# Row maximum negated by the masking operation, and the rotary product kept in the projection's PSUM bank

## The reference

```python
xn = layernorm(x)                                  # (4, 256, 512)
q = rope((xn @ wq).reshape(B, S, 32, 128), pos)    # 32 query heads
k = rope((xn @ wk).reshape(B, S, 8, 128), pos)     # 8 key/value heads, 4 query heads each
v = (xn @ wv).reshape(B, S, 8, 128)
scores = q @ k.T * 128 ** -0.5                     # per head
scores = where((j <= i) & (j > i - 128), scores, lowest)
s = (softmax(scores) @ v).reshape(B, S, 4096) @ wo
g = silu(w2(silu(xn @ W1.T) * (xn @ W3.T)))        # W1, W2, W3 from packed 4-bit values
out = x + s * g
```

## Time and profile before

| | |
|---|---|
| median of 3 runs | 923.35 us (922.11 to 925.94) |
| span of the profiled execution | 921.7 us |
| TensorE busy | 857.1 us, 93% |
| VectorE busy | 673.2 us, 73% |
| ScalarE busy | 471.5 us, 51% |
| GpSimd busy | 288.3 us, 31% |
| mean granted TensorE clock | 0.995 |

### The profile page before, as it was taken

How to read it: one execution, slowest core, us unless ns; L and a number is a source line. 1 busy time by engine, 2 the same in 40 slices (tenths; PEclk the granted TensorE clock), 3 DMA queues, 4 the chain that set the end, 5 groups by cost and what they waited for, 6 DMA issues and landing times.

```text
span 921.7 us, 14123 instructions
## 1 busy us (share of the span) xinstructions
PE 857.1 (93%) x4252; PEld 701.7 (76%) x4252; DVE 673.2 (73%) x1765; ACT 471.5 (51%) x1133; POOL 288.3 (31%) x223
## 2 busy tenths in 40 slices
PE   4999999999889998999999999989998999999877
PEld 3877888887677787878777777878787877778666
DVE  7954444425687969796978788597969787976994
ACT  2383112133675646565664756465747547564641
POOL 0153111124253222423321432043232314421862
PEclk9999999999999999999999999999999999999998
DMA  6100002002012001201010120012010201100111
GB/s 185 54 24 2 13 20 66 0 1 69 1 46 69 1 15 33 69 1 46 20 48 0 46 68 0 0 46 68 0 46 0 68 0 46 58 11 0 58 57 58
DMA packets 40224, 32.55 MB, mean 35 GB/s; under 512 B 5056, under 2 KB 32384, under 8 KB 40192
## 3 DMA queue, kind: packets, MB, share of 16 engines
q1 hardware_dynamic: 40192, 32.16, 12.0%
HBM read 30.05 MB, written 2.10 MB: 35 GB/s over the span
## 4 chain that ended last, share of the span: by engine, by line
PE 50%; DVE 33%; issue 11%; ACT 5%; DMA 1%; DVEq 0%; POOL 0%; ACTq 0%; SPq 0%
PE bank L992 15%; PE bank L994 15%; PE bank L993 15%; DVE probs L831 6%; DVE q L788 4%; DVE nmx L803 4%; DVE q L780 3%; DVE probs L819 3%; PE bank L1132 2%; DVE pl L837 2%; ACT oh L525 1%; DVE k L788 1%; DVE ol L848 1%; DVE ql L793 1%; DVE vl L842 1%
## 5 line engine op out<-in xcount | busy, mean ns | idle before, releaser
L322 POOL TENSOR_TENSOR swap<-swap,cst 128x512 f32<-128x512 f32 x80 | 106.8, 1334 | 369.7 <-ACT swap L485 369.7
L992 PE MATMUL bank<-xh,wih 128*128 128x512 f32 x384 | 159.3, 415 | 15.4 <-DVE q L780 15.4
L994 PE MATMUL bank<-xh,wil 128*128 128x512 f32 x384 | 151.0, 393 | 0.0
L993 PE MATMUL bank<-xl,wih 128*128 128x512 f32 x384 | 150.3, 392 | 0.0
L512 ACT ACTIVATE probs<-probs,nmx 128x128 f32<-128x128 f32 (+1 forms) x256 | 113.9, 446 | 57.1 <-DVE nmx L803 56.7
L992 PE MATMUL bank<-woh,oh 128*128 128x512 f32 x256 | 101.4, 396 | 10.3 <-DVE ol L848 10.3
L520 ACT ACTIVATE ph<-bank 128x512 fp32r<-128x512 f32 x96 | 55.6, 598 | 104.3 <-PE bank L1132 103.6
L831 DVE TENSOR_SCALAR probs<-probs,rinv 128x128 f32<-128x128 f32 (+1 forms) x256 | 99.4, 430 | 4.6
L994 PE MATMUL bank<-woh,ol 128*128 128x512 f32 x256 | 99.8, 390 | 0.0
L993 PE MATMUL bank<-wol,oh 128*128 128x512 f32 x256 | 99.7, 390 | 0.0
L992 PEld LDWEIGHTS bank<-xh,wih 128*128 128x128 f32 x384 | 72.2, 188 | 34.6 <-DVE q L780 14.5
(11 more groups left out here) (103 smaller groups left out, 1846.9 us busy)
## 6 DMA issues: line engine op xcount, KB each, us to landing
raw<-in_L_attn_wq SPq DMA_DIRECT2D x32, 256.0 KB, 2.8
raw<-in_L_attn_wo SPq DMA_DIRECT2D x32, 256.0 KB, 2.9
packed<-in_L_ffn_w SPq DMA_DIRECT2D x20, 128.0 KB, 2.1
xn<-in_L_attn_x SPq DMA_DIRECT2D x8, 256.0 KB, 3.6
raw<-in_L_attn_wk SPq DMA_DIRECT2D x8, 256.0 KB, 2.9
raw<-in_L_attn_wv SPq DMA_DIRECT2D x8, 256.0 KB, 2.6
raw<-in_L_attn_x SPq DMA_DIRECT2D x8, 256.0 KB, 2.7
out<-gate SPq DMA_DIRECT2D x8, 256.0 KB, 2.0
```

What stands on the lines that cost most here:

```text
L322: nc.gpsimd.tensor_tensor(v, v, spread(sin.unsqueeze(1), P, 2, SEQ), ALU.mult).then_inc(sin_done, 1)
L992: nc.tensor.matmul(out_, sh, mh, start=(i == 0), stop=False)
L993: nc.tensor.matmul(out_, sh, ml, start=False, stop=False)
L994: m = nc.tensor.matmul(out_, sl, mh, start=False, stop=(i == n - 1))
```

## The change

Two edits are made, both in the attention part.

The row maximum. The masking operation had scale 1, the maximum as reduction, and `NEG` as its start value. It now has scale minus `SM` (the softmax scale), the minimum as reduction, and `TOP` as start value, so that the masked scores stand in `probs` negated and scaled, and its accumulator is the bias itself. The exponential then has scale -1. `negate`, the tile `mx` and the semaphore `nmax_done` are gone; ScalarE waits for `masked`. Each head now has a memset of `pace`, where before each second one had it.

The rotary product. `cos_part` writes its product back into the projection's bank instead of into `q` or `k`. `rotate` reads the bank and `swap` and writes `q` or `k`. A projection that takes over the bank therefore waits for `rope_done`, the sum, where it waited for `cos_done`, the product.

```diff
+TOP = 3.0e38
...
             def exps(g, bp, b, h):
                 s = 4 * b + h
-                act.wait_ge(nmax_done, cnt(8, g, bp, s + 1))
+                act.wait_ge(masked, cnt(8, g, bp, s + 1))
                 for i, (c0, c1) in enumerate(((0, P), (P, 3 * P))):
                     e = nc.scalar.activation(probs[:, s, c0:c1], probs[:, s, c0:c1], ACT.Exp,
-                                             bias=nmx[:, s, i:i + 1], scale=SM, accum_out=rsum[:, s, i:i + 1])
+                                             bias=nmx[:, s, i:i + 1], scale=-1.0, accum_out=rsum[:, s, i:i + 1])
...
                 dve.wait_ge(swapped, cnt(5, g, bp, c + 1))
+                v = PJ_B[(c + 1 if c else 0) % 2][:, :].rearrange("p (b n) -> p b n", b=2)
+                nc.vector.tensor_tensor(v, v, spread(cos.unsqueeze(1), P, 2, SEQ), ALU.mult).then_inc(cos_done, 1)
+
+            def rotate(g, bp, c):
+                dve.wait_ge(sin_done, cnt(5, g, bp, c + 1))
+                dve.wait_ge(cos_done, cnt(5, g, bp, c + 1))
                 if c == 0:
                     wait(dve, scores_ps, cnt(8, g, bp, -8))
                 dst = q[:, c - 1, :] if c else k[:, bp, :]
-                nc.vector.tensor_tensor(dst.rearrange("p (b n) -> p b n", b=2),
-                                        PJ_B[(c + 1 if c else 0) % 2][:, :].rearrange("p (b n) -> p b n", b=2),
-                                        spread(cos.unsqueeze(1), P, 2, SEQ), ALU.mult).then_inc(cos_done, 1)
-
-            def rotate(g, bp, c):
-                dve.wait_ge(sin_done, cnt(5, g, bp, c + 1))
-                dve.wait_ge(cos_done, cnt(5, g, bp, c + 1))
-                dst = q[:, c - 1, :] if c else k[:, bp, :]
-                nc.vector.tensor_tensor(dst, dst, swap[:, (5 * bp + c) % 2, :], ALU.add).then_inc(rope_done, 1)
+                nc.vector.tensor_tensor(dst, PJ_B[(c + 1 if c else 0) % 2][:, :], swap[:, (5 * bp + c) % 2, :],
+                                        ALU.add).then_inc(rope_done, 1)
...
-            def negate(g, bp, b, h):
-
-                s = 4 * b + h
-                dve.wait_ge(masked, cnt(8, g, bp, s + 1))
-                nc.vector.tensor_scalar(nmx[:, s, :], mx[:, s, :], -SM, None, ALU.mult).then_inc(nmax_done, 1)
...
                     dve.wait_ge(scores_ps, cnt(8, g, bp, s + 1))
-                    if h > h0:
-                        negate(g, bp, b, h0)
-                    else:
-                        nc.vector.memset(pace[:, s // 2:s // 2 + 1], 0.0)
+                    nc.vector.memset(pace[:, s:s + 1], 0.0)
                     for i, (c0, c1) in enumerate(((0, P), (P, 3 * P))):
                         m = nc.vector.tensor_tensor_reduce(
-                            out=probs[:, s, c0:c1], in0=S_B[s % 2][:, c0:c1], in1=mask[:, c0:c1], scale=1.0,
-                            scalar=NEG, op0=ALU.add, op1=ALU.max, accum_out=mx[:, s, i:i + 1])
+                            out=probs[:, s, c0:c1], in0=S_B[s % 2][:, c0:c1], in1=mask[:, c0:c1], scale=-SM,
+                            scalar=TOP, op0=ALU.add, op1=ALU.min, accum_out=nmx[:, s, i:i + 1])
                     m.then_inc(masked, 1)
-                negate(g, bp, b, h0 + 1)
...
                     r = {0: -1, 1: 0, 2: 1, 4: 2, 5: 3}[c]
-                    wait(pe, cos_done, cnt(5, g, bp, r))
+                    wait(pe, rope_done, cnt(5, g, bp, r))
```

More of the change, by code:

```diff
@@ L119, in build @@
         vl = sb("vl", [P, 2, IT // P, HD], f32r, main)
-        mx = sb("mx", [P, 2 * GH, 2], f32, main)
-        pace = sb("pace", [P, 4], f32, main)
+        pace = sb("pace", [P, 2 * GH], f32, main)
         nmx = sb("nmx", [P, 2 * GH, 2], f32, main)
@@ L153, in build @@
         ffn_ps, ffn_read, gate_done = sem("ffn_ps"), sem("ffn_read"), sem("gate_done")
-        scores_ps, masked, nmax_done, exp_done, rinv_done, probs_done = (
-            sem("scores_ps"), sem("masked"), sem("nmax_done"), sem("exp_done"), sem("rinv_done"),
-            sem("probs_done"))
+        scores_ps, masked, exp_done, rinv_done, probs_done = (
+            sem("scores_ps"), sem("masked"), sem("exp_done"), sem("rinv_done"), sem("probs_done"))
         proj_ps, cos_done, swapped, sin_done, rope_done = (
```

## The result

The changed kernel takes 947.82 us (median of 4 runs, 946.93 to 950.8), the kernel before 924.55 in runs on the same chip: a ratio of 1.0263, interval 1.0237 to 1.0289, so 23 us slower; the forecast was 944. The profiled execution took 947.73 us with a span of 945.6.

The account below looks back on a forecast made before the run. TensorE was taken as the bound, busy 857.1 of 921.7 us. Narrow steps 16.4, wide 3.6, start 2.2, end -1 gave +21.2; with 921.7 and 1.65 around the span, 944 us, 8 in 10 for 929 to 962.

Parts of the forecast that it names:

- The three waits: Projects 2, 4 and 5 wait for rotary sums 0, 1 and 2: 1.0, 1.95 and 1.1 us late, 4.05 per step.
- The unblocked query sum: On VectorE, the query sum reading bank and swap takes 0.68 us instead of 1.28: 38 us less over 64.
- no late ol, pl or probabilities: In attend and output projection, waits for pl and ol go; 0.3 us for probabilities is kept in wide steps.
- The seven narrow steps: Steps with bp = 1: 4.05 us delay added, 1.7 removed, +2.35 each, times 7, 16.4 us.
- The wide steps: Steps with bp = 0: 4.05 + 0.3 us added, 3.9 removed, +0.45 each, times 8, 3.6 us.
- rival C: TensorE's clock falls too behind the longest wait: 1.5 us lost per step, 966 us in all; chance 10%.
- The start: Ahead of the first step: project 2 +1.5 us for the key sum, sums 1 and 2 another 0.7; 2.2.
- The end: Last group, without projections behind it: shorter VectorE work gives back an estimated 1 us.
- next to nothing of the 80 us: VectorE sheds some 80 of 673 us, but has slack, so next to nothing is on TensorE's path by itself.
- A: VectorE's relief wins: sums come early enough that new waits only replace the old cosine waits; 900 us, chance 6%.
- B: They balance: new waits of some 2.6 us per step, wide gains paying narrow losses; 922 to 928, chance 9%.
- D: Query sum still blocked: project 5 waits another 0.6 us, pl and ol stay late; 966 us, chance 4%.

Follow-up runs that it names:

- The early sums: The changed kernel with sum 0 issued ahead of both ol, sum 1 ahead of the last two normalises and vl, sum 2 ahead of pl: 885.02 us, ratio 0.9578.
- The mask edit alone: The kernel before with only the negations removed and the reduction turned round, rotary part as it was: 877.10 us, ratio 0.9489.
- the exchange of two instructions: The kernel before with vl and rotary sum 1 exchanged in VectorE's order, negations kept, nothing removed: 887.90 us, ratio 0.9604.
- the padding copy: The kernel before with negations removed and reduction turned round, plus one unread 128x512 VectorE copy per step ahead of vl: 909.01 us, ratio 0.9851.
- the rotary edit alone: The kernel before with product into the bank, sum from the bank and wait for the sum; negations as before: 972.25 us, ratio 1.0501.
- the waits alone: The kernel before with one line changed, projections waiting for rope_done (the sum) instead of cos_done (the product): 984.45 us, ratio 1.0649.

## Why the prediction was right, and what it missed

**The three waits: right.** The forecast was idle time near 0.8, 1.7 and 0.9 us ahead of projects 2, 4 and 5; the profile has 0.94 to 0.95, 1.77 to 1.78 and 0.87 to 0.96. The experiment with the one changed line shows that this edit brings them. The early sums show who sets each: the ol pair for the key sum, the last normalises and vl for sum 1 (its wait goes when it is issued ahead of them), pl for sum 2, whose wait falls to 0.40 when it goes ahead of pl (run only together with the other two).

**The unblocked query sum, no late ol, pl or probabilities: right.** 681 ns against 0.68 taken, and VectorE at 609.6 us against "near 595"; what I left out is kl, held in the sum's stead by (1061 - 706) x 16 = 5.7 us, the 64 further memsets, 3.8 us (priced below 0.1 each and then not added), and the normalises, 4.1 us longer in all. The product into PSUM at 696 ns stands by the lower of my two bounds.

**The terms.** I measured each step from the turns of v of one step to those of the next, before and after. The seven narrow steps went to 43.84 on average (forecast 43.7). Before they are not all alike: four took 41.3 and three 42.4, these with one more wait for ol of 0.8 to 0.9. So the term is 14.5 instead of 16.4 us; the sum was made on one narrow step, and the windows of all seven would have shown it. The earlier trace rows also leave out a wait of 0.29 us before project 4 in the wide steps. The wide steps (seven by this measure, the eighth lies in the end) cost 5.2 us where the forecast has 3.2 for seven. Five of them, at 43.8 to 44.0 us, are 0.1 to 0.4 longer. The other two took 45.3, with the clock at 0.96 over the step: rival C happened twice, at 1.4 us each, near the 1.5 priced. The start cost 2.8 (2.2 forecast), with the clock at 0.57 in 255 to 259 us, whose price no run separates. The end cost 1.5 where I had -0.6 (the eighth wide step's 0.45 less the 1 given back): the error there is in the sign, from the 5.32 us wait, 0.69 before, and the lower clock behind it. 2.8 + 14.5 + 5.2 + 1.5 = 24.0, and the spans differ by 945.6 - 921.7 = 23.9. The forecast of +21.2 is 2.7 us short of it. That it is so near is in part luck: the narrow steps cost 1.9 less than forecast, the two falls of the clock in the wide ones 2.8 more. The step lengths themselves, 43.84 and 43.8 to 44.0 against 43.7 and 44.0, are not luck.

**The step that failed without showing in the forecast** is the sentence that next to nothing of the 80 us taken from VectorE is on TensorE's path by itself. It was applied to the mask edit as much as to the query sums. Alone, that edit gives 46 us. Its neighbour failed with it, "46 us of removed negations don't help here, since ScalarE's exponentials set the last normalise": this holds in the changed kernel, but in the narrow step before, the exponentials ended at 650.89 and the last normalise's reciprocal started at 651.60, behind VectorE's own queue, and one held negation had delayed that queue. The numbers for it lay in my own rows: the sum starts 0.17 us behind the sine product, and its hold of 1 us is passed on to the next product, the pl and the ol, which are the waits of the earlier trace rows. I measured the delay that TensorE suffers as 1.7 and 3.9 us per step, so steps free of it would last 41.32 - 1.7 = 39.6 and 43.56 - 3.9 = 39.7. The mask edit alone gives 39.36 and 39.5. What I did not ask is how little it takes to remove it. Removing the negations brings VectorE to sum 1 by 1.16 us sooner and GpSimd to the sine product by only 0.53 (narrow step), and the sum wins the race by 0.46 to 0.48 us. Both directions are shown: the exchange of two instructions (37 us gained), and the padding copy (32 us lost).

So the rotary edit paid with a longer hold of the bank for what the other edit brings by itself. In the forecast's terms, it adds 4.05 us of delay per step to steps of 39.4, where I set it against the 1.7 and 3.9 that it removes; measured, 43.84 - 39.36 = 4.5 in a narrow step, and 4.4 in a wide one at full clock.

**Rivals.** A and B needed new waits below some 2.6 us per step; the measured ones give 4.4. D fell by the 681 ns. C was right in kind, for 2 steps of 14 and two places outside them.

## What to carry to other kernels

Before pricing an edit by the busy time that it removes, look for an instruction that starts a few tenths of a microsecond behind the one that holds it up. There a small shift, or an exchange of two instructions in the queue, can be worth many times the work removed, and it can tip back just as easily. A group's mean hides such holds: 364 ns stood here for negations of 0.17 us and held ones of up to 1.27, so ask for single instructions too. When a buffer's release moves from one instruction to a later one of the same engine, its price is all that stands between the two in the queue, and issuing the later one earlier gets most of it back.

## What the runs showed of the hardware

VectorE and GpSimd hold each other, and who starts second pays. Where the sum (two SBUF inputs) starts 0.17 or 0.11 us behind the sine product, it lasts 1.67 and 1.72 us and ends 0.5 us or more after it; where it starts 0.43 to 0.48 ahead, it lasts 0.68 and the sine product 1.42 and 1.35 instead of 1.29; where it starts only 0.06 ahead, still 0.68, and the sine product 1.76. The Trainium skill (SBUF — State Buffer, section Who interferes with whom) describes a pair of ports that these two engines share and lock for one another; the rows agree with it in kind. What decides it besides the order is where the inputs lie. In a narrow step of the changed kernel GpSimd's sine product runs from 577.04 to 578.32, and VectorE's timeline has:

```profile
577.16 0.68 DVE L777 TENSOR_TENSOR bank<-bank,cst 128x512 f32<-128x512 f32 x1
577.76 1.11 DVE L794 TENSOR_TENSOR kl<-k,kh 128x512 fp32r<-128x512 f32 x1
```

Both start while it runs. The one that works on PSUM and cos is not held, and kl, with two inputs in SBUF, is. With the rotary edit alone, query sums that read the bank start 0.15 to 0.18 us behind the sine product in eight steps and last 0.68. Small instructions with one tensor in SBUF are hit as hard as large ones: normalises of 128x128, a pair in 0.55 us elsewhere, took 2.63 beside two GpSimd operations in a row, and a negation of 128x2, 0.17 us elsewhere, took 1.26.

Waits of 1.77 us, with two of 0.9 beside them, in every step of 44 us left TensorE's granted clock at 1.00 in 12 of 14 steps, and in two let it fall (0.66 in 357 to 362 us). Longer waits went with more falls: with 3.9 us in each narrow step (the waits alone), it fell in all seven of them. What sets the two apart from their neighbours, no run here shows.
